# The second tail's scatters are put between its gathers, four groups behind

## The reference, cut to what matters

```
x = x + 0.5 * ffn(layernorm(x))      # attention over 16 tokens in 4 heads, then a mixture of 8 experts
x = x + attention(layernorm(x))      # causal, 16 heads of 16
x = x + 0.5 * ffn(layernorm(x))      # the same ffn with the same weights again
```

```
gates = softmax(y1 @ wg);  idx = argmax(gates)         # one expert of 8 for each row
loc   = place of the row among the rows of its expert
keep  = loc < 1024                                     # at most 1024 rows each, later ones are dropped
out   = keep ? gate * ((y1 @ w1[e] + b1[e]) @ w2[e] + b2[e]) : 0
y2    = layernorm(y1 + out) * ln2_g + ln2_b
```

## Time and profile before

| | |
|---|---|
| median of three runs | 2786.78 us (2779.59 to 2789.35) |
| the profiled execution, its own time | 2785.7 us |
| its span, first instruction to last | 2784.0 us |
| TensorE's mean granted clock | 0.928 |
| busy: PE, VectorE, ScalarE, GpSimd | 84%, 77%, 60%, 30% |
| mean DMA traffic | 101 GB/s |

### The profile page before, as it was taken

One profiled execution on the slowest core, in us unless ns is written; L12 is line 12 of the kernel. 1 busy time (PEld: TensorE's weight loads), 2 busy tenths in 40 slices (PEclk: granted clock), 3 DMA queues, 4 the chain that ended last, 5 costly groups with the idle time before them and its releaser, 6 DMA issues. The chain is left out here.

```text
span 2784.0 us, 46914 instructions
## 1 busy us (share of the span) xinstructions
PE 2344.2 (84%) x15864; PEld 1420.1 (51%) x15864; DVE 2148.9 (77%) x5653; ACT 1658.3 (60%) x3995; POOL 838.5 (30%) x853
## 2 busy tenths in 40 slices
PE   5999998867479959999999999999869999994263
PEld 4666665745345514444444444444646666663243
DVE  5888887727779868889898898987447888877067
ACT  3455453416534439999999999999315455452154
POOL 2343443264634420000000000000123343431746
PEclk8999999879789969999999999999989999996677
DMA  4132214372245464454554554542441121211722
GB/s 121 52 100 72 69 51 140 131 254 102 79 138 169 160 129 98 95 108 99 102 105 94 107 105 93 110 99 45 131 149 54 46 69 46 69 46 46 207 80 76
DMA packets 244687, 281.60 MB, mean 101 GB/s; under 512 B 41808, under 2 KB 212880, under 8 KB 243808
## 3 DMA queue, kind: packets, MB, share of 16 engines
q1 hardware_dynamic: 218192, 218.81, 30.7%
q0 software_dynamic: 16384, 50.35, 5.7%
q10 hardware_dynamic: 9872, 9.45, 1.0%
HBM read 190.63 MB, written 94.16 MB: 102 GB/s over the span
## 5 line engine op out<-in xcount | busy, mean ns | idle before, releaser
L2197 DVE CUSTOM_DVE_ANT_0 banks<-banks,attn_bias 128x128 f32<-128x128 f32 (+7 forms) x1024 | 760.1, 779 | 109.3 <-PE banks L1906 83.2
L2110 ACT ACTIVATE attn_probT<-banks 128x512 f32<-128x512 f32 x1152 | 623.6, 623 | 61.3 <-PE banks L1923 50.7
L1906 PE MATMUL banks<-attn_kst,attn_qst 96*128 96x512 bf16 (+3 forms) x1536 | 421.3, 336 | 23.1 <-DMA attn_kst<-kparts 13.0
L1923 PE MATMUL banks<-attn_qst,attn_kst 99*128 99x256 bf16 (+3 forms) x2176 | 411.6, 281 | 14.7 <-ACT attn_probT L2110 7.1
L1945 PE MATMUL banks<-attn_probT,attn_vb 128*32 128x256 f32 (+3 forms) x4352 | 316.2, 400 | 7.8 <-ACT attn_probT L2110 7.4
L1923 PEld LDWEIGHTS banks<-attn_qst,attn_kst 99*128 99x128 bf16 x2176 | 187.2, 97 | 169.6 <-ACT attn_probT L2110 55.5
L2255 POOL CAST attn_lowp<-attn_lowT 128x32 bf16<-128x32 f32 x64 | 13.5, 211 | 851.3 <-DVE attn_lowT L2205 851.3
L410 PE MATMUL banks<-ffn_xT,winT 128*128 128x512 f32 x512 | 250.9, 613 | 6.0 <-ACT ffn_w L610 2.9
L1906 PEld LDWEIGHTS banks<-attn_kst,attn_qst 96*128 96x128 bf16 x1536 | 117.4, 97 | 256.0 <-DVE attn_low L2197 158.5
L2098 ACT COPY banks<-attn_biasT 128x512 f32<-128x512 f32 x384 | 228.4, 630 | 28.5 <-DMA attn_biasT<-neardT 21.8
L870 POOL TENSOR_TENSOR ffn_xs<-ffn_xs,row_ffn_out 128x1024 f32<-128x1024 f32 x32 | 75.4, 2356 | 416.3 <-DVE ffn_xs L752 390.2
(11 more groups left out here) (254 smaller groups left out, 4500.2 us busy)
## 6 DMA issues: line engine op xcount, KB each, us to landing
rows<-ffn_xs SPq DMA_DIRECT2D x64, 512.0 KB, 3.1
attn_qst<-qparts SPq DMA_DIRECT2D x384, 64.0 KB, 2.8
attn_kst<-kparts SPq DMA_DIRECT2D x192, 128.0 KB, 4.9
ffn_xs<-in_L_ffn_w_dram SPq DMA_DIRECT2D x16, 1024.0 KB
attn_biasT<-neardT SPq DMA_DIRECT2D x128, 128.0 KB, 4.9
attn_bias<-neard SPq DMA_DIRECT2D x128, 128.0 KB, 2.2
qparts<-qkv_part SPq DMA_DIRECT2D x32, 384.0 KB, 2.8
kparts<-qkv_part SPq DMA_DIRECT2D x32, 384.0 KB, 2.8
```

The lines of the kernel that those rows point to most:

```text
L1906: mm = nc.tensor.matmul(score[k % 2][:, a:e], qst[0:K6, u, half, hh, ii * P:(ii + 1) * P], kst[0:K6, u, hh, a:e], start=True, stop=True)
L1923: mm = nc.tensor.matmul(tbank[t % 3][:, at:at + nb * P], kst[:, u, hh, j * P:(j + 1) * P], qst[:, u, half, hh, x:x + nb * P], start=(k == ...
L2110: nc.scalar.activation(probT[:, g % 2, i, 0:w], tbank[t % 3][:, 0:w], ACT.Exp, scale=-1.0).then_inc(s_exp, 1)
L2197: nc.vector.tensor_tensor_reduce(out=part, in0=part, in1=bias[:, hh, T - w:T], scale=1.0, scalar=BIG, op0=ALU.add, op1=ALU.min, accum_out= ...
```

## The change

A constant `LEAD` is 16 in turn 0, which gives the old order, and 4 in turn 1. There GpSimd's order becomes gather 0, 1, 2, 3, then gather 4, scatter 0, gather 5, scatter 1, ..., gather 15, scatter 11, and then scatter 12 to 15. Each scatter still waits for its `s_fin`. Nothing else changes; the numbers of gathers and scatters and their sizes stay.

```diff
+    LEAD = 4 if turn else NG
...
+            def scatter(n):
+                pool.wait_ge(s_fin, n + 1)
+                for t in range(GT):
+                    i = n * GT + t
+                    pool.indirect_dma_start(out, bass.IndirectOffsetOnAxis(ap=inv[:, i:i + 1], axis=0),
+                                            xs[:, n, t, 0:C], None).then_inc(s_sent, 16)
+
...
                 gather(n)
-            for n in range(NG):
-                pool.wait_ge(s_fin, n + 1)
-                for t in range(GT):
-                    i = n * GT + t
-                    pool.indirect_dma_start(out, bass.IndirectOffsetOnAxis(ap=inv[:, i:i + 1], axis=0),
-                                            xs[:, n, t, 0:C], None).then_inc(s_sent, 16)
+                if n >= LEAD:
+                    scatter(n - LEAD)
+            for n in range(NG - LEAD, NG):
+                scatter(n)
             pool.wait_ge(s_sent, sent0 + 16 * TILES)
```

## The result

The changed kernel takes 2810.12 us (median of 5, 2802.51 to 2813.0) against 2786.78 us (median of 5, 2779.59 to 2789.35): a ratio of 1.0077, 95% interval 1.0066 to 1.0089. Forecast were 2812 us, in a range of 2795 to 2841. The profiled execution took 2806.66 us, its span 2804.9.

What follows compares the result with a forecast made beforehand. It took the tail as bound by the gathers' 80 us, the recovery and VectorE's 16 groups. Gather 5 out at 2630.6, plus 5 x 26.7, 15.6 and 30.3, gave a 2810.0 span; with 1.7 and 1.1 added, 2812 us, range 2795 to 2841.

Steps and rivals of the forecast that it cites:

- gathers end to VectorE's going on: Second tail: VectorE recovers 3.5 us after the gathers pause at 2598.92, going on at 2602.5.
- fin(0): End of VectorE's scale(0) in the second tail, which the first scatter awaits: forecast at 2620.5, against 2673.51 before.
- landing: Second tail's loop: from the end of a group's fourth gather to the start of its place, 2.8 us.
- place(k+3) to fin(k): Second tail's loop: from placing group k+3 through transposes, products and sums to the end of scale(k), 12.8 us.
- fin(k) to G(k+5), meeting included: GpSimd from scale(k)'s end to the end of issuing gather k+5: 10.1 us, plus 1.0 for meeting VectorE's scaling.
- a pair: Second tail's loop: two groups share one chain of landing, passage and GpSimd's issuing, 26.7 us with one meeting.
- A: Rival: same chain in the second tail at its cheap end, full clock, no meetings, 2797.5 us; chance 0.14.
- B: Rival: GpSimd's own pace decides in the second tail, scatters find their fin ready, about 2775 us; chance 0.08.
- C: Rival: stops stay in the second tail's loop, each pair losing some 5 us, 2837 us; chance 0.12.
- D: Rival: gathers don't cause the stops; scale(0) still ends at 2673.5 and the loop adds on, 2865 us; chance 0.03.
- E: Rival: nothing measurable, early start and slower loop cancel, a pair of 21 to 22.5 us; chance 0.06.
- early start: Second tail: VectorE's scale(0) ends 53 us earlier because the gathers pause after group 4.

Runs made afterwards that it cites:

- order4: Changed kernel with, in the second tail, place(n+2) after normalise(n-1) on ScalarE and products before transposes on TensorE; 2736.1 us, 1.0067 of the kernel before.
- waits_only: Changed kernel's waits kept, but all scatters moved after the gathers; 2780.2 us, 1.0226 of the kernel before.
- lead5: Changed kernel with gathers five groups ahead of the scatters in place of four; 2727.0 us, 1.0035 of the kernel before; repeated at 2726.9 us.
- in B: Place of measurement where no traced run shows VectorE's stops; the kernel before takes 2715 to 2718 us, the changed one 2772.1 us, ratio 1.0203.
- in A: Place of measurement where VectorE's stops exist; the kernel before takes 2785 to 2787 us, the changed one 2810.1 us, repeated at 2810.6.
- paced: Kernel before, but each gather group of the second tail waits until the group before has landed; 2755.9 us, ratio 1.0150; repeated at 2756.4 us.
- lead8: Changed kernel with gathers eight groups ahead of the scatters in place of four; 2788.0 us, 1.0012 of the kernel before.

## Why the prediction was right

Point by point, from the first gather in both:

| step | forecast | measured |
|---|---|---|
| gathers end to VectorE's going on | 3.5 | 3.2 (2595.17 to 2598.38) |
| from there to fin(0) | 18 | 16.1 |
| fin(0) | 46.5 | 44.2 |
| landing | 2.8 | 2.7 (2652.81 to 2655.52) |
| place(k+3) to fin(k) | 12.8 | 13.3 (2655.52 to 2668.84) |
| fin(k) to G(k+5), meeting included | 11.1 | 11.1 (2668.84 to 2679.96) |
| a pair | 26.7 | 27.15 |
| last gather out | 190.1 | 191.4 |
| fin(12) to the last issue | 22.8 | 22.8 |
| span | 2810.0 | 2804.9 |

The chain was sized to within 1 us a pair, and the whole tail to 228.5 against 230.4. One term was wrong: the prediction let all be as before from fin(12) on, 30.3 us to the end of the span, and it took 27.0 (2777.90 to 2804.9), since the end came 3.3 us sooner after the last issue. With the tail's start, 3.7 us earlier, this outweighed the 1.9 that the tail took longer, and the median lay 3.5 above the profiled execution where 1.1 was added. That the forecast of 2812 missed by only 2 is thus partly luck; that the kernel became slower by 23 where 26 were forecast is not.

The one sum that carried it was the chain from a landed gather through place, transposes, products and scale. order4 shows that the place of gather k+3 in the engines' orders is in it, waits_only that the scatters aren't needed for it, lead5 that one more group ahead takes it away. All three were measured in B, where the changed kernel's pairs are as long as in A.

The meeting with VectorE's L1493 fell on a gather, not on a scatter: 1.87 us in place of 0.95, from 1.86 to 1.95 in the five pairs. No row before had shown a gather there. The Trainium skill's rule (SBUF — State Buffer, Who interferes with whom) is on a GpSimd instruction that reads SBUF beside a VectorE instruction with two SBUF inputs. These rows agree with it if a gather's indices count as such a read, as the prediction took them. The price isn't fixed: in the traces of before, changed, order4 and paced, each issue that started while L1487 (by its line there: L1493, L1495, L1498) ran ended 0.81 to 0.87 us after it, whether it had started 0.03 or 1.03 us into it. So an issue that starts late in such an operation loses little.

Rivals: A, the cheap end, would have had pairs of 24.9. B's place, a scatter that finds its fin ready, exists from five ahead on, and at four with order4's order; yet it brings no gain in B, where the kernel before hardly waits. C did not come in the changed kernel, but stops under a mixed stream do exist: lead8 has them. D is refuted by fin(0) at 44.2 and by the recovery 3.2 us after the gathers' end. E would have had pairs of 21 to 22.5.

The prediction said that the engines come back when the gathers pause. That holds for the end of the long stop only: the first, of 19.10 us, ended at 2618.93 while the gathers ran on to 2654.04.

What the prediction had not seen is how much rested on the place of measurement. Its early start (53 us forecast; 55.3 measured, each from its own first gather) was no property of the kernel: where nothing stops, fin(0) comes 9 us earlier still, but the tail of the kernel before is 36 to 40 us shorter, by the estimate above. The change's own price is the 57 us of B; in A more than half of it is paid back by stops that it avoids.

## What to carry to other kernels

- Before interleaving two streams on one queue, write down for the k-th item of the second which item of the first it really waits for, through every engine's order. If that one has just been issued, its whole latency (here 16 us) stands in the loop; one more item ahead, or one place less in an order, is worth more than any of the work.
- Divide that latency plus the queue's own time by the number of items that share it (26.2 / 2 here, / 3 at five ahead) and compare with the queue's own time per item (10.1). It turns where the first falls below the second.
- When engines stand still with their inputs there, measure in another place before counting that time as the kernel's.

## What the runs showed of the hardware

- In one kind of place VectorE, ScalarE and TensorE nearly stop after about 20 us of unbroken indirect DMA issue by GpSimd; VectorE stands for 17 to 19 us and then for 40 to 42. The first of these stops ends while the gathers still run, the second 6.5 to 7.7 us after they end. It is so at 103 GB/s as at 210, and lead8 has stops of 7.3 and 19.7 us with gathers and scatters mixed. In the other kind of place none of eight traces shows it, lead5's with over 100 us of mixed issue without a rest among them; the kernel before was not traced there. The cause is open.
- A gather of 128 rows holds GpSimd 0.95 us, with 0.30 between two, at 1 KB a row as at 2 KB.
- A gather or scatter of GpSimd that starts while VectorE scales 128x1024 float32 numbers (two SBUF inputs, 1.22 us) ends 0.81 to 0.87 us after that operation: up to 1.0 us longer than its 0.95 or 0.97, and the less the later it starts in it.
